# Regrouping the expert output matmuls of a windowed-attention and mixture-of-experts block: tiles in groups of 4 and 3

## The chip, the cores and the metric

The kernel runs on one core of a Trainium2 chip. The metric is device time in microseconds (us) of one execution. The engines are called by their names in the profile: PE is TensorE (PEld its weight loads), DVE is VectorE, ACT is ScalarE, POOL is GpSimd, SP is SyncE.

## What is computed

The input x is 32 images of 56 x 56 pixels with 96 channels. One block of a network is applied, cut here to what matters:

```python
# 1. attention in 7x7 windows of the shifted image, 12 heads of 8 channels
x = x + attention(ln(x)) @ w_proj.T + b_proj
# 2. mixture of 4 experts, the two best of each token, exact gelu
probs = softmax(ln(x) @ gate_w + gate_b); masked = top-2 of probs, renormalised
h = gelu(ln(x) @ w1[e] + b1[e])             # 96 -> 384, for each expert e
y = h @ w2[e] + b2[e]                       # 384 -> 96
x = x + sum over e of masked[e] * y[e]
```

All experts are computed for all tokens; the gate weighs their results. The change concerns y and the weighted sum.

## The kernel before

**Units.** A unit is a strip of two times 7 x 56 pixels: 784 tokens, 16 windows. There are 128 units, four to an image. Tokens lie on 112 partitions ("lanes") in 7 tiles of 112 tokens each. A loop step works on several units at once: `f` is the unit in its expert part, `a` the next one, in attention, `b` the one after, in its first norm and q/k/v. Each engine runs its own program in its own order, and semaphores tie them. Of the 128 steps, 127 have an `a`; the prologue runs the attention of unit 0 without any `f`.

**Order on PE in a step.** First the hidden layer of `f` (24 blocks of three matmuls, the first two of which belong to the step before). Then scores of pair 0 and eight passes n = 0 to 7, one for each pair of windows. A pass issues, in this order: `scores(n+1)`, `attend(n-1)`, `transpose_p(n)`, at n = 4 also `transpose1(b)` (7 transposes), then the expert groups that `GROUPS_AT[n]` lists, then `turn_o(n-1)`. At n = 0 some groups stand ahead of `scores(1)`. The last pair of each half, n + 1 = 3 and 7, has two mask matmuls more in its scores. Behind the passes come q/k/v of `b`, `project(a)`, the `LATE_GROUPS`, `transpose2(a)` with one q/k block of `b` in its middle, `hidden` blocks 0 and 1, and the gate's scores.

**Order on DVE in a pass.** `combine` of the groups in `COMBINES_AT[n]`, then `softmax_pair(n+1)` (row maximum L735, subtraction L739; it waits for `scores(n+1)`), then `normalise_o(n-1)` (reciprocal L746, product L750). PE's `turn_o(n-1)` waits for that product. At n = 1 to 3 DVE also does the statistics of a later unit's first norm. Behind the projection `residual` runs: residual sums and statistics of both parts (4 and 3 tiles), centring and scaling (L779, L786), on which `transpose2` waits, the low parts of the normed input `x2_low` (L814), and four combines among them.

**An expert group.** `experts(f, g)` multiplies n tiles of tokens with w2 of one expert. Each tile takes 9 matmuls of 96 columns (three chunks of 128 hidden channels, three products of high and low float16 parts: L1123, L1125, L1127), ahead of them stands one matmul for the bias, n x 96 columns wide (L1116). The result lies in the PSUM bank `Y_BANK[g]`; a group waits until the group before it in that bank has been combined. Groups of expert 0 need low parts made by DVE, later experts those made by POOL (`lo_done`). `combine(f, g)` on DVE (L891) multiplies by the gate into a slot of `y_gated` (four slots), `add` on POOL (L458) adds the slot to the residual, and `store` on SP waits for the last add. POOL's step lists the low parts L448, adds and the first norm in a fixed order. `PARTS` is the number of groups of an expert, `N_Y` that of a unit.

**Other waits on groups.** `transpose1(b)` waits for `gated` at 6, since it writes banks 5 and 6. `hidden` block 1 writes bank 7 and waits for `gated` at 11. ACT's `round_chunk` writes a slot of `g_hi` anew once the expert that read it is done (`PARTS * (chunk // CPE - 1)` groups).

Of the kernel before, what the change touches and what calls it, by code (L numbers as in the profile page):

```python
# [33 lines left out]
B, IMG, C = 32, 56, 96  # L34
# [6 lines left out]
EXPERTS, HID = 4, 384  # L41
CHUNKS = EXPERTS * HID // 128
CPE = HID // 128
# [3 lines left out]
LANES = 2 * IMG  # L47
# [9 lines left out]
def at(unit, per_unit, k=0):  # L57

    m, c = unit
    return m * (UPI * per_unit) + (c * per_unit + k)  # L60
# [39 lines left out]

GROUP_TILES = ((0, 2), (2, 2), (4, 3))
PARTS = len(GROUP_TILES)
GROUPS_AT = ((0, 1, 2), (3,), (4,), (5,), (), (6,), (7,), ())
COMBINES_AT = ((0, 1), (2,), (3,), (4,), (5,), (), (6,), (7,))
LATE_GROUPS = (8, 9, 10, 11)
STATS_AT = ((), (0, 1), (2, 3), (4, 5, 6), (), (), (), ())
ROUND_AT = ((), (6,), (7,), (8,), (), (9,), (10,), (11,))

# [1 line left out]
T1_AT = 4  # L112
X1_LOW_AT = ((), (), (), (), (), (0, 1), (2, 3), ())

Y_BANK = (5, 7, 6, 5, 7, 6, 7, 7, 7, 4, 7, 4)
B2_COLS = EXPERTS * 3 * C

N_T1, N_QK, N_V, N_S, N_PT, N_O, N_OT = 2, 4, 2, 8, 16, 8, 2
VW = HD + 1
# [3 lines left out]
N_PROJ, N_T2, N_H, N_Y = 2, 2, 24, PARTS * EXPERTS  # L123
# [15 lines left out]
def build(nc, x, packed, wp, consts, out, keys):  # L139
    ctx = ExitStack()  # L140
    with ctx:
        def sb(name, shape, dt=F32):
            return ctx.enter_context(nc.sbuf_tensor(name, shape, dt))
# [86 lines left out]
        g_sb = sb("g_sb", [128, CHUNKS, TOK])  # L230
        g_hi = sb("g_hi", [128, 2 * CPE, TOK + PAD], F16)
        g_lo = sb("g_lo", [128, 2 * CPE, TOK + PAD], F16)
        y_gated = sb("y_gated", [LANES, 4, 3 * C])


        s_const = sem("s_const")
# [169 lines left out]
        @block.gpsimd  # L406
        def _(pool):

            nc.gpsimd.memset(k_bd[:, :, :, :], 0.0).then_inc(s_zero, 1)
            nc.gpsimd.memset(v_bd[:, :, :], 0.0).then_inc(s_zero, 1)  # L410
            nc.gpsimd.memset(p_sb[:, :, :, :], 0.0).then_inc(s_zero, 1)
            for odd in range(2):
                pool.wait_ge(s_zero, 3 + odd)
                nc.gpsimd.memset(v_bd[NB * odd:NB * odd + WW, :, VW * odd + HD:VW * (odd + 1)], 1.0
                                 ).then_inc(s_zero, 1)

            def norm1(a):

                u = a[1] % UPI
                pool.wait_ge(var1_done, at(a, 1, 1))  # L420
                nc.gpsimd.tensor_tensor(rstd1[:, :], ve1[:, :], minus_half[0:LANES, :].broadcast_to([LANES, W]),
                                        ALU.pow).then_inc(rstd1_done, 1)
                if not first(a):
                    pool.wait_ge(t1_done, at(a, N_T1))
                wide = [LANES, W, C]
                nc.gpsimd.tensor_tensor(xn1[:, :, :], xa[:, u, :].rearrange("p (t c) -> p t c", c=C),
                                        mv1[:, :, 0:1].broadcast_to(wide), ALU.subtract
                                        ).then_inc(centre1_done, 1)
                pool.wait_ge(rstd1_done, at(a, 1, 1))
                pool.wait_ge(centre1_done, at(a, 1, 1))  # L430
                nc.gpsimd.tensor_tensor(xn1[:, :, :], xn1[:, :, :], rstd1[:, :].unsqueeze(2).broadcast_to(wide),
                                        ALU.mult).then_inc(norm1_done, 1)

            def rsqrt2(f):
                for k, (j0, n) in enumerate(((0, 4), (4, 3))):
                    pool.wait_ge(var2_done, at(f, 2, k + 1))
                    nc.gpsimd.tensor_tensor(rstd2[:, j0:j0 + n], ve2[:, j0:j0 + n],  # L437
                                            minus_half[0:LANES, :].broadcast_to([LANES, n]),
                                            ALU.pow).then_inc(rstd2_done, 1)

            def low_part(f, chunk):

                if chunk < 2 * CPE:
                    pool.wait_ge(hi_dve, at(f, N_ROUND, chunk + 1))
                else:
                    pool.wait_ge(hi_act, at(f, N_ROUND, chunk - 2 * CPE + 1))
                slot = chunk % (2 * CPE)
                nc.gpsimd.tensor_tensor(g_lo[:, slot, 0:TOK], g_sb[:, chunk, :], g_hi[:, slot, 0:TOK],  # L448
                                        ALU.subtract).then_inc(lo_done, 1)

            def add(f, u, g):

                e, j0, n = tiles_of(g)
                pool.wait_ge(gated, at(f, N_Y, g + 1))
                if g >= PARTS:
                    pool.wait_ge(comb_done, at(f, N_Y, g - PARTS + 1))
                slot = xr[:, u, j0 * C:(j0 + n) * C]
                nc.gpsimd.tensor_tensor(slot, y_gated[:, g % 4, 0:n * C], slot, ALU.add).then_inc(comb_done, 1)  # L458

            def prologue():  # L460
                pool.wait_ge(s_ready, 1)
                norm1((0, 0))
                norm1((0, 1))
                rsqrt2((0, 0))

            def step(f, a, b, u):
                for chunk in range(CPE, 2 * CPE):
                    low_part(f, chunk)
                for g in range(3):
                    add(f, u, g)  # L470
                if b is not None:
                    norm1(b)
                for chunk in range(2 * CPE, 3 * CPE):
                    low_part(f, chunk)
                    add(f, u, chunk - CPE)
                low_part(f, 9)
                low_part(f, 10)
                add(f, u, 6)
                low_part(f, 11)
                add(f, u, 7)  # L480
                if a is not None:
                    rsqrt2(a)

                    pool.wait_ge(norm2_done, at(a, 2, 2))
                for g in LATE_GROUPS:
                    add(f, u, g)

            schedule(pool, step, prologue)


# [138 lines left out]
        def _(dve):  # L629
# [124 lines left out]
            def residual(f, before=None):  # L754
# [37 lines left out]
                sums_of(*first_part)  # L792
                variances(*first_part)
                if before is not None:
                    combine(before, 8)
                sums_of(*second_part)
                if before is not None:
                    combine(before, 9)
                centre(*first_part)
                variances(*second_part)  # L800
                scale(*first_part)
# [1 line left out]
                scale(*second_part)  # L803
                x2_low(f, 0)
                if before is not None:
                    combine(before, 10)
                    combine(before, 11)
                x2_low(f, 1)

            def x2_low(f, k):  # L810
# [148 lines left out]
        def _(pe):  # L959
# [143 lines left out]
            def experts(f, g):  # L1103

                e, j0, n = tiles_of(g)
                if e == 0:
                    pe.wait_ge(lo_dve, at(f, CPE, CPE))
                else:
                    pe.wait_ge(lo_done, at(f, N_LO, CPE * e))
                if g < 3:  # L1110
                    pe.wait_ge(gelu_done, at(f, N_H, N_H - 2 + g))
                earlier = [i for i in range(g) if Y_BANK[i] == Y_BANK[g]]
                if earlier:
                    pe.wait_ge(gated, at(f, N_Y, max(earlier) + 1))
                y = y_bank(g)[:, 0:n * C]
                T.matmul(y, ones16[:, :], b2_16[:, e * 3 * C:e * 3 * C + n * C], start=True, stop=False,  # L1116
                         skip_group_check=True)
                for k in range(n):
                    cols = slice((j0 + k) * LANES, (j0 + k) * LANES + 128)
                    for c in range(CPE):  # L1120
                        slot, wc = e % 2 * CPE + c, slice((e * CPE + c) * C, (e * CPE + c + 1) * C)
                        outp = y[:, k * C:(k + 1) * C]
                        T.matmul(outp, g_hi[:, slot, cols], w2_hi[:, wc], start=False, stop=False,  # L1123
                                 skip_group_check=True)
                        T.matmul(outp, g_hi[:, slot, cols], w2_lo[:, wc], start=False, stop=False,  # L1125
                                 skip_group_check=True)
                        ins = T.matmul(outp, g_lo[:, slot, cols], w2_hi[:, wc], start=False,  # L1127
                                       stop=(c == CPE - 1), skip_group_check=True)
                ins.then_inc(y_done, 1)
# [11 lines left out]
            def attention(a, b, f=None):  # L1141


                for n in range(8):
                    groups = list(GROUPS_AT[n]) if f is not None else []
                    if n == 0 and groups:
                        experts(f, groups.pop(0))
                        experts(f, groups.pop(0))
                    if n < 7:
                        scores(a, n + 1)  # L1150
                    if n:
# [4 lines left out]
                    if n == T1_AT and b is not None:  # L1156
                        if f is not None:

                            pe.wait_ge(gated, at(f, N_Y, 6))
                        transpose1(b)  # L1160
                    for g in groups:
                        experts(f, g)
# [15 lines left out]
                hidden(a, (0,))  # L1178
                if f is not None:

                    pe.wait_ge(gated, at(f, N_Y, 11))
                hidden(a, (1,))
                gate_scores(a)

# [23 lines left out]
def _layout(w_qkv, b_qkv, w_proj, b_proj, rel_table, gate_w, gate_b, w1, b1, w2, b2):  # L1208
# [4 lines left out]
    wg = np.concatenate([gate_w, gate_b[None]], 0)  # L1213
    w1b = np.concatenate([w1.transpose(1, 0, 2).reshape(C, EXPERTS * HID), b1.reshape(1, -1)], 0)
    b2r = np.zeros((128, B2_COLS), f)
    b2r[0] = b2r[32] = np.repeat(b2, 3, 0).reshape(-1)

    col, row = np.arange(WW) // W, np.arange(WW) % W
    idx = (row[:, None] - row[None] + W - 1) * (2 * W - 1) + (col[:, None] - col[None] + W - 1)
# [54 lines left out]
```

## Time and profile before

| | |
|---|---|
| time, median of 3 runs | 6585.76 us (6585.39 to 6585.8) |
| time of the profiled run | 6582.02 us |
| its span, first to last instruction | 6580.2 us |
| PE busy | 6329.5 us, 96% of the span |
| PEld busy | 5075.5 us, 77% |
| DVE busy | 5021.6 us, 76% |
| ACT busy | 4719.7 us, 72% |
| POOL busy | 3763.3 us, 57% |
| DMA | mean 44 GB/s, hardware queue 14.4% of 16 engines |
| mean granted TensorE clock | 0.996 |

A steady step lasts 50.40 us, from one `scores(0)` (3004.69) to the next (3055.09). A row of the timeline has the start, the duration, the engine, the line of the kernel, and what was written from what; an "xcount" merges rows of one kind; a bracket at the end gives the idle time before it and what ended that. Matmul durations overlap, so PE's progress is read from the difference of two starts, not from a duration. A row of the view of stretches has the stretch, its length, the busy time and instruction count of PE, PEld, DVE, ACT and POOL, PE's granted clock, the DMA share and the GB/s.

### The profile page before, as it was taken

Reading aid. Unit: us, or ns where it says so; the run is one execution under the profiler, and the core shown is the slowest. Engines: PE = TensorE matmul, PEld = TensorE weight load, DVE = VectorE, ACT = ScalarE, POOL = GpSimd, SP = SyncE. Lnnn points to the kernel's source line nnn. Section 1 sums busy time; section 2 is a strip of 40 time slices with the busy share of each in tenths; the row PEclk is TensorE's granted clock in tenths of the full one; section 3 lists DMA queues with packets and bytes.
Section 4 is the critical chain, followed back from the end, with each engine's and each line's share of the span. In section 5 each row is a group of like instructions: output and inputs, shape, how many; then the busy total and the mean of one; then the engine's idle time right before and its main releaser. Section 6 shows DMA issues by size and latency. Waiting matters only on the chain.

```text
span 6580.2 us, 265098 instructions
## 1 busy us (share of the span) xinstructions
PE 6329.5 (96%) x99456; PEld 5075.5 (77%) x99456; DVE 5021.6 (76%) x15655; ACT 4719.7 (72%) x9087; POOL 3763.3 (57%) x3337
## 2 busy tenths in 40 slices
PE   5999999999999999999999999999999999999997
PEld 4777777777777777777777777777777777777776
DVE  5777777777777777777777777777777777777775
ACT  3777777777777777777777777777777777777775
POOL 2565555555555565556555555555565555555555
PEclk9999999999999999999999999999999999999999
DMA  1111111111111111111111111111111111111110
GB/s 57 44 43 44 46 45 43 44 46 44 45 42 46 44 44 44 45 43 44 44 46 43 44 45 45 43 45 45 44 43 45 46 44 43 44 46 45 45 41 24
DMA packets 190611, 290.00 MB, mean 44 GB/s; under 512 B 42450, under 2 KB 151634, under 8 KB 189266
## 3 DMA queue, kind: packets, MB, share of 16 engines
q1 hardware_dynamic: 189394, 273.23, 14.4%
q8 instruction: 831, 13.62, 0.9%
q14 instruction: 386, 3.16, 0.2%
HBM read 138.18 MB, written 77.07 MB: 33 GB/s over the span
## 4 chain that ended last, share of the span: by engine, by line
PE 73%; DVE 15%; issue 5%; ACT 4%; POOL 2%; SPq 1%; DVEq 0%; DMA 0%; ACTq 0%; POOLq 0%
PE ps_t L1036 10%; PE ps_o L1053 9%; PE ps_f L964 8%; PE ps_f L965 8%; PE ps_f L966 8%; PE ps_s L1016 5%; PE ps_s L1026 4%; PE ps_f L1127 3%; PE ps_f L1125 3%; PE ps_f L1123 3%; DVE s_max L735 3%; PE ps_o L1062 3%; POOL rstd L437 2%; DVE stat L766 2%; PE ps_t L983 2%
## 5 line engine op out<-in xcount | busy, mean ns | idle before, releaser
L448 POOL TENSOR_TENSOR g_lo<-g_sb,g_hi 128x784 f16<-128x784 f32 x1152 | 2014.9, 1758 | 1774.3 <-DVE g_hi L873 1013.8
L541 ACT ACTIVATE g_sb<-ps_f 128x392 f32<-128x392 f32 x3072 | 1525.9, 497 | 127.6 <-PE ps_f L966 126.8
L563 ACT ACTIVATE pt_sb<-ps_t 113x588 f32<-113x588 f32 x1024 | 677.4, 662 | 1077.8 <-PE ps_t L1036 1065.0
L735 DVE TENSOR_REDUCE s_max<-ps_s 113x12 f32<-113x588 f32 x1024 | 789.1, 771 | 746.9 <-PE ps_s L1026 746.9
L1127 PE MATMUL ps_f<-w_hi,g_lo 128*128 128x96 f16 x8832 | 1227.3, 206 | 0.0
L1125 PE MATMUL ps_f<-w_lo,g_hi 128*128 128x96 f16 x8832 | 1226.7, 206 | 0.0
L1123 PE MATMUL ps_f<-w_hi,g_hi 128*128 128x96 f16 x8832 | 1226.1, 206 | 0.0
L458 POOL TENSOR_TENSOR xr<-y_gated,xr 112x192 f32<-112x192 f32 (+1 forms) x1536 | 987.0, 660 | 374.6 <-DVE y_gated L891 275.7
L964 PE MATMUL ps_f<-x_hi,w_hi 128*128 128x392 f16 x3072 | 1012.2, 329 | 19.5 <-issue 5.3
L965 PE MATMUL ps_f<-x_lo,w_hi 128*128 128x392 f16 x3072 | 1010.7, 329 | 0.0
L966 PE MATMUL ps_f<-x_hi,w_lo 128*128 128x392 f16 x3072 | 1010.6, 329 | 0.0
L1036 PE MATMUL ps_t<-ident,p_sb 113*113 113x113 f32 x6144 | 854.6, 275 | 26.9 <-ACT p_sb L558 26.7
L1125 PEld LDWEIGHTS ps_f<-w_lo,g_hi 128*128 128x128 f16 x8832 | 862.9, 98 | 10.2
L1123 PEld LDWEIGHTS ps_f<-w_hi,g_hi 128*128 128x128 f16 x8832 | 865.2, 98 | 0.1
L1127 PEld LDWEIGHTS ps_f<-w_hi,g_lo 128*128 128x128 f16 x8832 | 863.5, 98 | 0.0
L739 DVE TENSOR_TENSOR s_sub<-ps_s,s_max 113x588 f32<-113x588 f32 x1024 | 790.0, 772 | 57.0
L1053 PEld LDWEIGHTS ps_o<-v_bd,pt_sb 113*49 113x49 f32 x24576 | 738.0, 125 | 114.1 <-ACT pt_sb L563 67.1
L1053 PE MATMUL ps_o<-v_bd,pt_sb 113*49 113x18 f32 x24576 | 785.5, 198 | 24.2 <-ACT pt_sb L563 20.2
L558 ACT ACTIVATE p_sb<-s_sub 113x588 f32<-113x588 f32 x1024 | 715.7, 699 | 77.6 <-DVE s_sub L739 72.6
L1036 PEld LDWEIGHTS ps_t<-ident,p_sb 113*113 113x113 f32 x6144 | 695.9, 178 | 80.4 <-issue 51.3
L534 ACT ACTIVATE g_hi<-g_sb 128x784 f16<-128x784 f32 x768 | 647.3, 843 | 3.1 <-PE ps_f L1127 3.1
L437 POOL TENSOR_TENSOR rstd<-ve,cst 112x4 f32<-112x4 f32 (+1 forms) x256 | 270.9, 1058 | 595.4 <-DVE ve L775 595.4
(132 smaller groups left out, 13415.6 us busy)
## 6 DMA issues: line engine op xcount, KB each, us to landing
k_bd<-keys SPq DMA_DIRECT2D x1536, 36.8 KB
q_st<-qk_hi SPq DMA_DIRECT2D x768, 49.0 KB, 1.9
xr<-x SPq DMA_DIRECT2D x224, 139.1 KB
out<-xr SPq DMA_DIRECT2D x224, 139.1 KB
xa<-x SPq DMA_DIRECT2D x224, 136.5 KB
keys<-qk_hi SPq DMA_DIRECT2D x128, 147.0 KB, 2.4
keys<-qk_lo SPq DMA_DIRECT2D x128, 147.0 KB, 2.8
q_st<-qk_lo SPq DMA_DIRECT2D x384, 49.0 KB, 2.0
```

The source lines that it names most:

```text
L448: nc.gpsimd.tensor_tensor(g_lo[:, slot, 0:TOK], g_sb[:, chunk, :], g_hi[:, slot, 0:TOK], ALU.subtract).then_inc(lo_done, 1)
L458: nc.gpsimd.tensor_tensor(slot, y_gated[:, g % 4, 0:n * C], slot, ALU.add).then_inc(comb_done, 1)
L541: nc.scalar.activation(g_sb[:, chunk, half * STRIP:(half + 1) * STRIP], h_bank[k % 3][:, 0:STRIP], ACT.Gelu, scale=1.0 / WSCALE).then_inc( ...
L735: V.tensor_reduce(s_max[:, :], scores, AX.X, ALU.max).then_inc(max_done, 1)
L964: T.matmul(outp, lhs_hi, rhs_hi, start=start, stop=False, skip_group_check=True)
L965: T.matmul(outp, lhs_hi, rhs_lo, start=False, stop=False, skip_group_check=True)
L966: return T.matmul(outp, lhs_lo, rhs_hi, start=False, stop=True, skip_group_check=True)
L1036: ins = T.transpose(bank[2 + p // 4][0:SPAN, (p % 4) * 128:(p % 4) * 128 + SPAN], p_sb[0:SPAN, n % 2, 2 * p:2 * p + 2, :].rearrange("p h k ...
L1053: ins = T.matmul(ps_o[NB * s:NB * s + WW, O0 + p * 2 * VW:O0 + (p + 1) * 2 * VW], pt_sb[0:SPAN, p, s * WW:(s + 1) * WW], v_bd[0:SPAN, win ...
L1123: T.matmul(outp, g_hi[:, slot, cols], w2_hi[:, wc], start=False, stop=False, skip_group_check=True)
L1125: T.matmul(outp, g_hi[:, slot, cols], w2_lo[:, wc], start=False, stop=False, skip_group_check=True)
L1127: ins = T.matmul(outp, g_lo[:, slot, cols], w2_hi[:, wc], start=False, stop=(c == CPE - 1), skip_group_check=True)
```

## The change

Each expert's 7 tiles are split into two groups, of 4 and 3 tiles, instead of three groups of 2, 2 and 3. A unit has 8 groups instead of 12. The number of tiles within the pairs stays at 18, that behind the projection at 10. By pass n = 0 to 7, the tiles were 7, 2, 2, 3, 0, 2, 2, 0 and become 7, 4, 3, 0, 0, 4, 0, 0; of the 7 at n = 0, 4 stand ahead of `scores(1)` in both. Behind the projection groups of 3, 2, 2 and 3 tiles become 3, 4 and 3. DVE's combines and POOL's adds follow; the combine that stood between the residual statistics of the second part and the centring of the first is gone from there, and the two behind the first `x2_low` have 4 and 3 tiles in place of 2 and 3. The semaphore counts, banks, the slots of `y_gated` and the layout of the bias follow.

```diff
--- before.py
+++ after.py
@@ -100,11 +100,11 @@
 
 
 
-GROUP_TILES = ((0, 2), (2, 2), (4, 3))
+GROUP_TILES = ((0, 4), (4, 3))
 PARTS = len(GROUP_TILES)
-GROUPS_AT = ((0, 1, 2), (3,), (4,), (5,), (), (6,), (7,), ())
-COMBINES_AT = ((0, 1), (2,), (3,), (4,), (5,), (), (6,), (7,))
-LATE_GROUPS = (8, 9, 10, 11)
+GROUPS_AT = ((0, 1), (2,), (3,), (), (), (4,), (), ())
+COMBINES_AT = ((0,), (1,), (2,), (3,), (), (), (4,), ())
+LATE_GROUPS = (5, 6, 7)
 STATS_AT = ((), (0, 1), (2, 3), (4, 5, 6), (), (), (), ())
 ROUND_AT = ((), (6,), (7,), (8,), (), (9,), (10,), (11,))
 
@@ -112,8 +112,8 @@
 T1_AT = 4
 X1_LOW_AT = ((), (), (), (), (), (0, 1), (2, 3), ())
 
-Y_BANK = (5, 7, 6, 5, 7, 6, 7, 7, 7, 4, 7, 4)
-B2_COLS = EXPERTS * 3 * C
+Y_BANK = (5, 7, 6, 5, 7, 7, 4, 7)
+B2_COLS = EXPERTS * 4 * C
 
 N_T1, N_QK, N_V, N_S, N_PT, N_O, N_OT = 2, 4, 2, 8, 16, 8, 2
 VW = HD + 1
@@ -230,7 +230,7 @@
         g_sb = sb("g_sb", [128, CHUNKS, TOK])
         g_hi = sb("g_hi", [128, 2 * CPE, TOK + PAD], F16)
         g_lo = sb("g_lo", [128, 2 * CPE, TOK + PAD], F16)
-        y_gated = sb("y_gated", [LANES, 4, 3 * C])
+        y_gated = sb("y_gated", [LANES, 4, 4 * C])
 
 
         s_const = sem("s_const")
@@ -466,18 +466,17 @@
             def step(f, a, b, u):
                 for chunk in range(CPE, 2 * CPE):
                     low_part(f, chunk)
-                for g in range(3):
-                    add(f, u, g)
+                add(f, u, 0)
                 if b is not None:
                     norm1(b)
+                add(f, u, 1)
                 for chunk in range(2 * CPE, 3 * CPE):
                     low_part(f, chunk)
-                    add(f, u, chunk - CPE)
-                low_part(f, 9)
-                low_part(f, 10)
-                add(f, u, 6)
-                low_part(f, 11)
-                add(f, u, 7)
+                add(f, u, 2)
+                add(f, u, 3)
+                for chunk in range(3 * CPE, CHUNKS):
+                    low_part(f, chunk)
+                add(f, u, 4)
                 if a is not None:
                     rsqrt2(a)
 
@@ -792,10 +791,8 @@
                 sums_of(*first_part)
                 variances(*first_part)
                 if before is not None:
-                    combine(before, 8)
+                    combine(before, 5)
                 sums_of(*second_part)
-                if before is not None:
-                    combine(before, 9)
                 centre(*first_part)
                 variances(*second_part)
                 scale(*first_part)
@@ -803,8 +800,8 @@
                 scale(*second_part)
                 x2_low(f, 0)
                 if before is not None:
-                    combine(before, 10)
-                    combine(before, 11)
+                    combine(before, 6)
+                    combine(before, 7)
                 x2_low(f, 1)
 
             def x2_low(f, k):
@@ -1113,7 +1110,7 @@
                 if earlier:
                     pe.wait_ge(gated, at(f, N_Y, max(earlier) + 1))
                 y = y_bank(g)[:, 0:n * C]
-                T.matmul(y, ones16[:, :], b2_16[:, e * 3 * C:e * 3 * C + n * C], start=True, stop=False,
+                T.matmul(y, ones16[:, :], b2_16[:, e * 4 * C:e * 4 * C + n * C], start=True, stop=False,
                          skip_group_check=True)
                 for k in range(n):
                     cols = slice((j0 + k) * LANES, (j0 + k) * LANES + 128)
@@ -1145,7 +1142,6 @@
                     groups = list(GROUPS_AT[n]) if f is not None else []
                     if n == 0 and groups:
                         experts(f, groups.pop(0))
-                        experts(f, groups.pop(0))
                     if n < 7:
                         scores(a, n + 1)
                     if n:
@@ -1156,7 +1152,7 @@
                     if n == T1_AT and b is not None:
                         if f is not None:
 
-                            pe.wait_ge(gated, at(f, N_Y, 6))
+                            pe.wait_ge(gated, at(f, N_Y, 4))
                         transpose1(b)
                     for g in groups:
                         experts(f, g)
@@ -1178,7 +1174,7 @@
                 hidden(a, (0,))
                 if f is not None:
 
-                    pe.wait_ge(gated, at(f, N_Y, 11))
+                    pe.wait_ge(gated, at(f, N_Y, 8))
                 hidden(a, (1,))
                 gate_scores(a)
 
@@ -1213,7 +1209,7 @@
     wg = np.concatenate([gate_w, gate_b[None]], 0)
     w1b = np.concatenate([w1.transpose(1, 0, 2).reshape(C, EXPERTS * HID), b1.reshape(1, -1)], 0)
     b2r = np.zeros((128, B2_COLS), f)
-    b2r[0] = b2r[32] = np.repeat(b2, 3, 0).reshape(-1)
+    b2r[0] = b2r[32] = np.repeat(b2, 4, 0).reshape(-1)
 
     col, row = np.arange(WW) // W, np.arange(WW) % W
     idx = (row[:, None] - row[None] + W - 1) * (2 * W - 1) + (col[:, None] - col[None] + W - 1)
```

## Rows read from the trace of the kernel before

**Rows 1.** Busy time by stretch: steady unit, then prologue pairs; columns in the text above.
```profile
3004.69:3055.09 50.40, 49.32 (x780) 39.56 (x779) 39.09 (x122) 36.88 (x72) 29.25 (x27) 1.00 0.15 44
89.00:101.50 12.50, 10.17 (x176) 8.39 (x176) 9.92 (x33) 7.00 (x15) 0.00 (x0) 1.00 0.01 3
```
**Rows 2.** Timeline, TensorE, steady unit, pairs 1 to 6: start us, duration us, engine, line.
```profile
3010.10 0.44 PE L1016 MATMUL ps_s<-bias,sel 128*64 128x392 f16 x4
...
3011.94 0.25 PE L1116 MATMUL ps_f<-b,ones 128*128 128x192 f16 x1
...
3013.14 0.36 PE L1016 MATMUL ps_s<-bias,sel 128*64 128x392 f16 x2
...
3015.24 0.25 PE L1116 MATMUL ps_f<-b,ones 128*128 128x192 f16 x1
...
3016.43 0.45 PE L1016 MATMUL ps_s<-bias,sel 128*64 128x392 f16 x4
...
3018.27 0.29 PE L1116 MATMUL ps_f<-b,ones 128*128 128x288 f16 x1
...
3019.54 0.27 PE L1062 MATMUL ps_o<-turn,o_tok 113*96 113x113 f32 x1
...
3019.74 0.45 PE L1016 MATMUL ps_s<-bias,sel 128*64 128x392 f16 x4
...
3022.78 0.44 PE L1016 MATMUL ps_s<-bias,sel 128*64 128x392 f16 x4
...
3024.86 0.25 PE L1116 MATMUL ps_f<-b,ones 128*128 128x192 f16 x1
...
3025.70 0.26 PE L1062 MATMUL ps_o<-turn,o_tok 113*96 113x113 f32 x1
...
3025.90 0.36 PE L1016 MATMUL ps_s<-bias,sel 128*64 128x392 f16 x2
...
3029.19 0.73 PE L1053 MATMUL ps_o<-v_bd,pt_sb 113*49 113x18 f32 x24
```
**Rows 3.** Timeline, TensorE, the prologue's pairs without expert groups.
```profile
89.04 0.45 PE L1016 MATMUL ps_s<-bias,sel 128*64 128x392 f16 x4
...
91.85 0.30 PE L1062 MATMUL ps_o<-turn,o_tok 113*96 113x113 f32 x1 [0.81 <-DVE o_tok L750]
...
92.08 0.44 PE L1016 MATMUL ps_s<-bias,sel 128*64 128x392 f16 x4
...
98.17 0.36 PE L1016 MATMUL ps_s<-bias,sel 128*64 128x392 f16 x2
...
101.22 0.30 PE L1062 MATMUL ps_o<-turn,o_tok 113*96 113x113 f32 x1 [0.80 <-DVE o_tok L750]
...
101.46 0.32 PE L1053 MATMUL ps_o<-v_bd,pt_sb 113*49 113x18 f32 x6
```
**Rows 4.** Timeline, VectorE, steady unit, pair 3: normalised output of pair 2.
```profile
3018.93 0.26 DVE L750 TENSOR_TENSOR o_tok<-ps_o,s_rec 113x96 f32<-113x96 f32 x1
```
**Rows 5.** Timeline, GpSimd, steady unit: last low part of expert 2.
```profile
3020.54 1.68 POOL L448 TENSOR_TENSOR g_lo<-g_sb,g_hi 128x784 f16<-128x784 f32 x1 [0.16 <-ACT g_hi L534]
```
**Rows 6.** Timeline, VectorE, steady unit, behind the projection.
```profile
3038.83 0.34 DVE L891 TENSOR_TENSOR y_gated<-ps_o,gate 112x192 f32<-112x192 f32 x1
...
3041.79 0.62 DVE L814 TENSOR_TENSOR x_lo<-ps_f,x_hi 96x448 f16<-96x448 f32 x1
...
3042.59 0.44 DVE L891 TENSOR_TENSOR y_gated<-ps_o,gate 112x288 f32<-112x288 f32 x1
...
3042.96 0.49 DVE L814 TENSOR_TENSOR x_lo<-ps_f,x_hi 96x336 f16<-96x336 f32 x1
```
**Rows 7.** Timeline, TensorE, steady unit, behind the late groups.
```profile
3040.59 0.59 PE L1079 MATMUL ps_f<-ident,xn 112*96 112x112 f32 x4
...
3042.97 0.33 PE L964 MATMUL ps_f<-x_hi,w_hi 128*128 128x392 f16 x1
...
3043.51 0.18 PE L964 MATMUL ps_s<-wg_hi,x_hi 128*128 128x4 f16 x1
```

## Prediction

> **What bounds the kernel now.** I read the busy times of one steady unit first. PE is busy 49.32 us of the unit's 50.40 us, DVE 39.09, ACT 36.88, POOL 29.25 [rows 1]. So PE sets the pace and only two things can move the time: how long PE needs for its instructions, and where it stands still between them. The second view is PE's timeline of the passes over the window pairs, read from start to start. It shows two kinds of pass. Some are as long as PE's own instructions; others are as long as a chain through DVE. That chain goes `scores(n+1)` on PE, row maximum and subtraction on DVE, reciprocal and product of the pair before on DVE, `turn_o(n-1)` on PE. In pass 3 it starts at 3016.43 [rows 2] and ends at 3018.93 + 0.26 = 3019.19 [rows 4], 2.76 us on. `turn_o` starts only at 3019.54 [rows 2], because the expert group of three tiles before it lasts longer. Here the chain is covered, by 0.35 us. The third view is the most telling one. The prologue runs the same passes without any expert group, so it shows the chain bare: from 89.04 to 91.85 PE gets to `turn_o` 2.81 us after the scores, having stood idle 0.81 us for the DVE product, and the next scores start at 92.08 [rows 3]. A pass without a group therefore lasts 3.04 us. With mask matmuls in its scores it lasts 3.29 us (98.17 to 101.46), with 0.80 us idle [rows 3].
>
> **The change, part by part.** First the price of a group on PE. Three tiles last 3019.54 - 3018.27 = 1.27 us, two tiles 3025.70 - 3024.86 = 0.84 us [rows 2]. A tile is 0.43 us and nothing measurable is left for the start of a group (0.84 less two tiles is -0.02). Four tiles are 1.27 + 0.43 = 1.70 us. Four bias matmuls a unit fewer, of the same columns in sum, are worth nothing by these rows; with the rounding of 0.02 us each, at most 0.08 us a unit, which is left to the range.
>
> Now the passes, each as (scores to group) + group + `turn_o`, the last being 0.20 us (3019.54 to 3019.74) [rows 2], and compared with the pass of before:
>
> - Pass 0: seven tiles in both kernels, four of them ahead of `scores(1)`: 0.
> - Pass 1, 2 tiles become 4. Scores to group is 3011.94 - 3010.10 = 1.84 us. New length 1.84 + 1.70 + 0.20 = 3.74. Old: 3013.14 - 3010.10 = 3.04. This is +0.70, less than two tiles (0.86), because the old pass was already waiting for the chain.
> - Pass 2, 2 become 3. Scores to group is 3015.24 - 3013.14 = 2.10 us. New 2.10 + 1.27 + 0.20 = 3.57, old 3016.43 - 3013.14 = 3.29: +0.28.
> - Pass 3, 3 become 0. Old 3019.74 - 3016.43 = 3.31. PE's own work in it would be 1.84 + 0.20 = 2.04, but the chain holds it at 3.04 [rows 3]: -0.27. Of 1.27 us of group taken out, 1.00 us becomes idle time.
> - Pass 4 has the transposes of the next unit and no group in either: 0.
> - Pass 5, 2 become 4. Scores to group is 3024.86 - 3022.78 = 2.08 us. New 2.08 + 1.70 + 0.20 = 3.98, old 3025.90 - 3022.78 = 3.12: +0.86.
> - Pass 6, 2 become 0. Old 3029.19 - 3025.90 = 3.29 [rows 2]. Bare, by the prologue, 3.29 [rows 3]: 0. The old pass was already at the chain's length, so taking the group out gives nothing.
> - Pass 7 has no group in either: 0.
>
> The passes sum to 0.70 + 0.28 - 0.27 + 0.86 = +1.57 us a unit [rows 2, 3]. The same tiles are done in the same order, but two passes now lack cover and stand at the chain, and their tiles lengthen passes that had nothing left to hide.
>
> Behind the projection PE's groups take the same ten tiles. The old fourth group had to wait for a combine on DVE; the new third one needs a combine that DVE does before it, so that stall goes. What is late next is the norm. `transpose2` starts at 3040.59 [rows 7], as soon as DVE has scaled. One combine of two tiles, at 3038.83, disappears from ahead of the centring: 0.34 us long, some 0.25 us from its start to the next instruction's [rows 6]. So `transpose2`, and the first `x2_low` behind it, come 0.25 us earlier, the latter at 3041.79 - 0.25 = 3041.54. But the tiles of that combine are done elsewhere. Between the start of `x2_low` and that of the last combine there are 3042.59 - 3041.79 = 0.80 us [rows 6]; two tiles more in the combine between them cost 0.10 us each by 0.34 us for two tiles and 0.44 us for three [rows 6], so the last combine starts at 3041.54 + 0.80 + 0.20 = 3042.54 and ends 0.44 us later, at 3042.98. This is what `hidden` block 1 now waits for, where before it waited for the smaller combine ahead of it. It started at 3042.97 and the gate's scores at 3043.51 [rows 7]; now it can start at about 3043.04, adding 0.05 us from a DVE end to PE (the chain ends 2.76 us after the scores, PE goes on 2.81 us after them). The second `x2_low` starts as before, within 0.04 us of 3042.96. So the 0.25 us are given back: I take +0.05 us a unit, between -0.25 (the head start stays) and +0.30 (a combine of four tiles, at most 0.54 us by the same slope, held against the 0.25).
>
> What costs nothing, and its cover: DVE has four combines fewer a unit and PE does not wait for DVE there; a combine of four tiles at passes 1, 2 and 6 stands ahead of the row maximum, which waits for scores anyway, and both engines have room in the unit [rows 1]. POOL's adds are four fewer. Its first norm moves ahead of two adds, three low parts of expert 2 come in a row ahead of two adds. The last of these low parts ended at 3020.54 + 1.68 = 3022.22 [rows 5], and the group that reads them started at 3024.86 [rows 2]: 2.6 us spare. ACT's rounding, which releases that low part, moves back 0.98 us with passes 1 and 2, the group only 0.71 us, and 2.3 us stay. If that cover were gone the group of pass 5 would wait, with PE's queue behind it. No wait is added on SP and no transfer is issued, moved or resized; the stores only follow the last add.
>
> Sum: 1.57 + 0.05 = 1.62 us a unit, in the 127 steps that have passes: 205.7 us. The last step, without passes, I take as unchanged. Against the profiled run 6582.02 + 205.7 = 6787.7 us. The median of the runs lies 3.7 us above the profiled run, which gives 6791 us, 3.1% slower.
>
> **A rule that bears on it.** In the prologue's passes, PE idled 0.8 us out of every 3.04 to 3.29 us and its granted clock read 1.00, the 2.4 GHz level [rows 1, 3]. The Trainium skill (TensorE: Matmul & The Clock Gate, "A second HAM failure mode: psum-queue depth-cycling") tells of a kernel in which frequent short idle times between groups of matmuls made the clock swing between its two levels. By that rule the new idle times would cost clock, which is rival 4 below; the row speaks against it.
>
> **The rivals.**
> (1) The chain is no bound: `turn_o` would be released earlier in passes 3 and 6, which then shrink to PE's own work, 2.04 us and 2.10 + 0.23 = 2.33 us. Pass 3 would give -1.27 and pass 6 -0.96, the passes in sum 0.70 + 0.28 - 1.27 + 0.86 - 0.96 = -0.39, with the late part -0.34 us a unit: 6586 - 43 = 6543 us, 0.7% faster than before. It decides when the DVE product of a bare pass ends less than 2.0 us after its scores start. For it speaks only that DVE is at 78% load; against it the two waits of 0.8 us in rows 3. Chance 0.04.
> (2) The head start behind the projection stays, because PE or ACT hides the later combines: 1.57 - 0.25 = 1.32 us a unit, 6586 + 168 = 6753 us. It would need block 1 of `hidden` not to wait for the last combine. Chance 0.09.
> (3) The late combines cost more, +0.30 us: 1.87 x 127 = 237, 6823 us. Chance 0.04.
> (4) The clock falls to 1.2 GHz behind the bare pass 3 and stays there for passes 4 and 5: these last 3.04 and 3.98 us, and at half the clock at most twice that, an estimate: +7.0 us a unit, 127 x 7.0 = 889, 7475 us. Chance 0.01.
> (5) The cover moves without net effect, the new idle time being offset by the stalls that go; that would need 1.6 us of old stalls in a unit that has 50.40 - 49.32 = 1.08 us of idle in all [rows 1]. Chance 0.02.
>
> **How the numbers follow.** The forecast, 6791 us, has 0.80; its own error of about 0.1 us a unit is 13 us either way. Range: from rival 2 less a little for the bias matmuls, 6750, to rival 3, 6825; left out are rivals 1, 4 and 5 and some error, some 0.1. A difference of 0.2% (13 us) is about what a measurement can tell from no change. Faster has 0.04 (rival 1), same 0.02 (rival 5), slower the rest, 0.94.
>
> **What would show it.** In the profile after: idle of about 1.0 us before `turn_o` released by the DVE product, twice a unit, in passes 3 and 6, so some 250 us of such waits in all; pass lengths 3.74, 3.57, 3.04, 3.04, 3.98, 3.29 us; a unit of 52.0 us; the late groups without a wait between them; `hidden` block 1 waiting for the last combine; clock still 1.00. The prediction is wrong if passes 3 and 6 are shorter than 3.0 us, if passes 1 or 5 grow by less than 0.6 us, or if a wait on POOL's low parts appears ahead of the group of pass 5.

## The result, and the profile after

The changed kernel takes 6783.29 us (median of 4 runs, 6783.15 to 6785.4) against 6585.78 us for the kernel before on the same chip (6585.39 to 6586.61): a ratio of 1.030, 95% interval 1.0283 to 1.0318. It is 198 us slower; 205 us were forecast.

From the page of the changed kernel, the span and the busy times:

```profile
span 6781.3 us, 261146 instructions
...
PE 6329.8 (93%) x98944; PEld 5024.2 (74%) x98944; DVE 5042.8 (74%) x15143; ACT 4717.4 (70%) x9087; POOL 3697.3 (55%) x2825
```

PE is busy for 6329.8 us, where it was 6329.5 us: its work is the same, and the whole loss is time in which it stands still. A steady unit in the view of stretches (length, busy PE, PEld, DVE, ACT, POOL, clock, DMA share, GB/s), to be read beside [rows 1]:

```profile
3044.92:3096.89 51.97, 49.28 (x775) 39.14 (x774) 39.20 (x118) 36.85 (x72) 29.17 (x24) 1.00 0.15 43
```

The unit has grown by 1.57 us (50.40 to 51.97), PE's busy time in it not at all. Over 127 units that is 199 us. Every fourth unit, in which the loop closes, is 0.32 us longer in both kernels. The passes, on PE's timeline of two neighbouring units (start, duration), to be read beside [rows 2]:

```profile
3050.32 0.45 PE L1013 MATMUL ps_s<-bias,sel 128*64 128x392 f16 x4
...
3052.16 0.33 PE L1113 MATMUL ps_f<-b,ones 128*128 128x384 f16 x1
...
3053.85 0.26 PE L1059 MATMUL ps_o<-turn,o_tok 113*96 113x113 f32 x1
3054.05 0.36 PE L1013 MATMUL ps_s<-bias,sel 128*64 128x392 f16 x2
...
3057.61 0.44 PE L1013 MATMUL ps_s<-bias,sel 128*64 128x392 f16 x4
...
3060.43 0.30 PE L1059 MATMUL ps_o<-turn,o_tok 113*96 113x113 f32 x1 [0.81 <-DVE o_tok L749]
3060.66 0.45 PE L1013 MATMUL ps_s<-bias,sel 128*64 128x392 f16 x4
...
3063.70 0.45 PE L1013 MATMUL ps_s<-bias,sel 128*64 128x392 f16 x4
```
```profile
3011.35 0.44 PE L1013 MATMUL ps_s<-bias,sel 128*64 128x392 f16 x4
...
3015.32 0.36 PE L1013 MATMUL ps_s<-bias,sel 128*64 128x392 f16 x2
...
3018.38 0.30 PE L1059 MATMUL ps_o<-turn,o_tok 113*96 113x113 f32 x1 [0.80 <-DVE o_tok L749]
3018.61 0.73 PE L1050 MATMUL ps_o<-v_bd,pt_sb 113*49 113x18 f32 x24
```

The lengths are 3.73, 3.56, 3.05 and 3.04 us for passes 1 to 4 (first fence, scores to scores), 3.97 and 3.29 us for passes 5 and 6 (second fence). The two brackets are the bare chain of [rows 3] in the steady unit: 0.81 us idle in pass 3, 0.80 us in pass 6, each ended by the DVE product. In the sums of waits (total us, times, longest), the two rows on this product were, before and then after:

```profile
PEld ps_o L1062 <- DVE o_tok L750: 50.3, 133, 1.0
PE ps_o L1062 <- DVE o_tok L750: 3.8, 6, 0.8
...
PEld ps_o L1059 <- DVE o_tok L749: 300.4, 387, 1.0
PE ps_o L1059 <- DVE o_tok L749: 208.4, 260, 0.8
```

The weight load of `turn_o` (PEld) waited once a unit before, for 0.4 us; two waits a unit of 1.0 us are new. The matmul itself (PE) hardly waited before and now waits twice a unit for 0.8 us, 204.6 us more in all. PE's idle time as a whole (span less busy time) grew by 200.8 us, from 250.7 to 451.5: these waits are the loss. Behind the projection, PE's timeline, beside [rows 7]; `project` started at 3023.88, in the unit of the old rows at 3034.46. The first row below is from before, the others from after:

```profile
3034.46 1.61 PE L1068 MATMUL ps_f<-wp_sb,o_sb 128*112 128x96 f32 x14
...
3023.88 1.61 PE L1065 MATMUL ps_f<-wp_sb,o_sb 128*112 128x96 f32 x14
...
3029.76 0.59 PE L1076 MATMUL ps_f<-ident,xn 112*96 112x112 f32 x4
...
3032.46 0.34 PE L961 MATMUL ps_f<-x_hi,w_hi 128*128 128x392 f16 x1 [0.16 <-DVE y_gated L888]
...
3032.97 0.17 PE L961 MATMUL ps_s<-wg_hi,x_hi 128*128 128x4 f16 x1
```

Counted from `project`, `transpose2` starts 0.25 us earlier (5.88 us in place of 6.13), block 1 of `hidden` 0.07 us later (8.58, was 8.51), the gate's scores 0.04 us later (9.09, was 9.05). The bracket names what took the head start back: the last late combine. The sums of waits balance here: the late group's wait for a combine (23.2 us, 127 times) is gone, and block 1's wait for the last combine (20.0 us, 127 times) is new.

### The profile page after: what moved, and what is told of

Same layout as the page of the kernel before. It is cut to its first block, busy times and chain, and to the rows that moved or that the text cites. A ratio compares the mean times of both kernels' runs of the same rounds, so it can differ in the third digit from the quotient of the medians.

```text
span 6781.3 us, 261146 instructions
## 1 busy us (share of the span) xinstructions
PE 6329.8 (93%) x98944; PEld 5024.2 (74%) x98944; DVE 5042.8 (74%) x15143; ACT 4717.4 (70%) x9087; POOL 3697.3 (55%) x2825
## 4 chain that ended last, share of the span: by engine, by line
PE 65%; DVE 20%; issue 8%; ACT 4%; POOL 2%; DMA 0%; DVEq 0%; SPq 0%; ACTq 0%; POOLq 0%
PE ps_f L961 8%; PE ps_f L963 7%; PE ps_f L962 7%; PE ps_t L1033 7%; PE ps_o L1050 6%; DVE s_max L734 6%; PE ps_s L1013 5%; PE ps_s L1023 4%; PE ps_f L1124 3%; PE ps_f L1122 3%; PE ps_f L1120 3%; PE ps_o L1059 3%; POOL rstd L437 2%; DVE stat L765 2%; PE ps_t L980 2%
## 5 line engine op out<-in xcount | busy, mean ns | idle before, releaser
L1124 PE MATMUL ps_f<-w_hi,g_lo 128*128 128x96 f16 x9216 | 1248.1, 206 | 0.0
L1122 PE MATMUL ps_f<-w_lo,g_hi 128*128 128x96 f16 x9216 | 1247.6, 206 | 0.0
L1120 PE MATMUL ps_f<-w_hi,g_hi 128*128 128x96 f16 x9216 | 1247.2, 206 | 0.0
L458 POOL TENSOR_TENSOR xr<-y_gated,xr 112x384 f32<-112x384 f32 (+1 forms) x1024 | 907.1, 896 | 411.3 <-DVE y_gated L888 295.7
L1122 PEld LDWEIGHTS ps_f<-w_lo,g_hi 128*128 128x128 f16 x9216 | 901.9, 98 | 39.1
L1120 PEld LDWEIGHTS ps_f<-w_hi,g_hi 128*128 128x128 f16 x9216 | 903.3, 98 | 0.1
L1124 PEld LDWEIGHTS ps_f<-w_hi,g_lo 128*128 128x128 f16 x9216 | 902.1, 98 | 0.0
L888 DVE TENSOR_TENSOR y_gated<-ps_f,gate 112x288 f32<-112x288 f32 (+1 forms) x896 | 445.5, 497 | 232.2 <-PE ps_f L1124 231.8
```

## Experiments

Every ratio is against the kernel before, measured on the same chip: its median was 6585.6 us beside the first four, 6587.6 us beside the next three, 6586.7 us beside the last. The edits are shown shortened (banks, counts, combines and adds follow the groups): the first, second and fourth against the kernel before, the third and sixth against the changed kernel, the fifth against the fourth, the last against the seventh.

### Placement without large groups

```diff
-GROUPS_AT = ((0, 1, 2), (3,), (4,), (5,), (), (6,), (7,), ())
-LATE_GROUPS = (8, 9, 10, 11)
+GROUPS_AT = ((0, 1, 2), (3, 4), (5,), (), (), (6,), (), ())   # expert 2: 4 and 3 tiles, the others 2, 2, 3
+LATE_GROUPS = (7, 8, 9, 10)
```

> Only the placement of the changed kernel: passes 0 to 7 have 7, 4, 3, 0, 0, 4, 0, 0 tiles, but the groups stay small: the four tiles of pass 1 are two groups of two, the three late groups of expert 3 stay 2, 2 and 3 (only expert 2 has 4 and 3, since its four tiles of pass 5 find one free bank). The part behind the projection is that of before. If the loss comes from where the tiles stand (my theory), the passes last 3.73, 3.56, 3.05, 3.04, 3.97 and 3.29 us (passes 1 to 6), +1.55 us a unit over before, and the time is 6586 + 197 = 6783 us, within 5 us. If it comes from the size of the groups (wider bias matmuls, combines and adds), most of the 198 us is absent: under 6650 us.

Measured: 6793.0 us (5 runs, 6790.9 to 6797.4), ratio 1.0316 (1.0302 to 1.0330). The pass lengths are 3.73, 3.56, 3.05, 3.04, 3.97 and 3.29 us, those of the changed kernel to 0.01 us, and a unit lasts 51.95 us. Pass 1 in its timeline, now with two groups of two tiles:

```profile
3002.29 0.25 PE L1119 MATMUL ps_f<-b,ones 128*128 128x192 f16 x1
...
3003.14 0.25 PE L1119 MATMUL ps_f<-b,ones 128*128 128x192 f16 x1
...
3003.99 0.27 PE L1065 MATMUL ps_o<-turn,o_tok 113*96 113x113 f32 x1
```

Two groups of two last 1.70 us, as one of four does (3052.16 to 3053.85, 1.69 us). The placement alone makes the whole loss, and with 11 groups in place of 8 nothing of it comes back. The size of the groups was varied in pass 1 and behind the projection and is worth nothing in pass 1; pass 5 kept its group of four, so there it was not tested. The time itself is 10 us above the expected 6783, beyond the 5 us allowed: the units that are not disturbed are as expected, and what is added is told under the next experiment.

### One move: pass 6 to pass 5

```diff
-GROUPS_AT = ((0, 1, 2), (3,), (4,), (5,), (), (6,), (7,), ())
+GROUPS_AT = ((0, 1, 2), (3,), (4,), (5,), (), (6,), (), ())   # group 6 has four tiles
```

> One move alone: the two tiles of pass 6 are done in pass 5, joined with the two there; passes 1 to 3 and the part behind the projection as before. My theory: pass 6 was already at the length of the chain (3.29 us) and gives nothing back, pass 5 goes from 3.12 to 3.97 us: +0.85 us x 127 = 108 us, 6694 us. If a pass without a group shrank to PE's own work, pass 6 would give back 0.96 us: 6586 - 14 = 6572 us.

Measured: 6707.8 us (4 runs, 6705.0 to 6710.6), ratio 1.0185 (1.0169 to 1.0200): +122 us, where 108 were expected and -14 by the rival. Passes 1 to 6 last 3.04, 3.29, 3.31, 3.04, 3.97 and 3.29 us: pass 5 grew by 0.85 us and pass 6 gave nothing back. An undisturbed unit lasts 51.26 us, +0.86, which makes 109 us. The other 13 us are not in the passes. Stretches of this kernel, an ordinary unit and one that isn't, then single microseconds in the second:

```profile
3063.89:3115.15 51.26, 49.37 (x777) 39.45 (x777) 39.07 (x121) 36.85 (x72) 29.11 (x26) 1.00 0.15 43
...
3217.99:3270.63 52.64, 50.91 (x777) 40.53 (x777) 39.16 (x121) 36.85 (x72) 29.58 (x27) 0.97 0.15 43
```
```profile
3242.00:3243.00 1.00, 0.31 (x4) 0.12 (x2) 0.96 (x3) 0.66 (x2) 0.09 (x1) 1.00 0.01 5
3243.00:3244.00 1.00, 0.90 (x26) 0.76 (x26) 0.62 (x3) 1.00 (x3) 0.00 (x0) 1.00 0.04 8
3244.00:3245.00 1.00, 1.00 (x8) 0.74 (x5) 0.49 (x2) 0.33 (x1) 0.59 (x1) 0.55 0.00 0
3245.00:3246.00 1.00, 1.00 (x7) 1.00 (x6) 0.28 (x1) 0.49 (x1) 1.00 (x1) 0.50 0.00 0
```

In 3242 to 3243 PE stands idle for 0.80 us, waiting for the product in pass 6; one microsecond later the granted clock reads 0.55 and then 0.50, the 1.2 GHz level, for 3.4 us in all, and this unit lasts 1.38 us longer. From unit 1 to unit 126 of this kernel the clock falls so in 10 units, in the kernel above in 7, in the next one in 4, in the changed kernel in one (unit 45). Ten times 1.38 us are 14 us, the missing 13; seven times are 10 us, what the experiment above had too much. Each of these 22 falls comes 1.7 to 2.1 us after the start of the wait of 0.80 us in pass 6, none behind a bare pass 2 or 3. In the same part the kernel before has a single fall, in unit 125, behind an idle time of 1.7 us, and the kernels of the later experiments, which have no such wait in pass 6, have none. So the long wait in pass 6 goes with the falls; why only a few of these waits are followed by one, and why their number differs between kernels with the same passes, stays open. The Trainium skill (TensorE: Matmul & The Clock Gate, "A second HAM failure mode: psum-queue depth-cycling") tells of a kernel in which frequent short idle times between groups of matmuls make the clock swing between its two levels. These rows agree in so far as the clock falls behind a short idle time, but in 10 of 127 units at most.

### The same tiles spread evenly

```diff
-GROUPS_AT = ((0, 1), (2,), (3,), (), (), (4,), (), ())
+GROUPS_AT = ((0, 1), (2,), (), (3,), (), (4,), (), ())
```

> The changed kernel with its group of three tiles moved from pass 2 to pass 3, so that groups stand in passes 1, 3 and 5, evenly. My theory: what counts is how many passes have no group at all, each of which leaves about 0.96 us idle; there are two either way, so the sum of the passes is 3.73 + 3.29 + 3.31 + 3.04 + 3.97 + 3.29 us against 3.73 + 3.56 + 3.05 + 3.04 + 3.97 + 3.29 us, the same within 0.02 us: 6782 us, within 5 us of the changed kernel. Rival: an even spread lets the engines recover between groups, which should be worth a part of the loss, 6700 to 6760 us.

Measured: 6788.0 us (5 runs, 6786.2 to 6792.2), ratio 1.0309 (1.0295 to 1.0323), as the changed kernel. Passes 1 to 6 last 3.73, 3.29, 3.31, 3.04, 3.97 and 3.29 us, the unit 51.96 us. Pass 2 gave up 0.27 us and pass 3 took it. The even spread is worth nothing: three groups in the five passes 1, 2, 3, 5 and 6 leave two bare in either order. (Which of them are bare was varied only between 2 and 3.) The 5 us above the changed kernel are at the edge of what was expected; this kernel's four falls of the clock, at 1.38 us, account for them.

### The part behind the projection alone

```diff
-                if before is not None:
-                    combine(before, 9)
                 centre(*first_part)
...
-                    combine(before, 10)
-                    combine(before, 11)
+                    combine(before, 9)    # four tiles
+                    combine(before, 10)   # three tiles
```

> Only the part behind the projection as in the changed kernel: groups and passes of before, but expert 3 has groups of 4 and 3, late groups are 3, 4 and 3 tiles and the combine between the statistics and the centring is gone. My theory: transpose2 starts 0.25 us earlier, and hidden block 1 waits for the last combine and gives it back: +0.04 us a unit, 6591 us, 6586 to 6596. Rival (the head start stays): -0.25 us a unit, 6554 us.

Measured: 6585.5 us (11 runs, 6583.6 to 6589.2), ratio 1.0000 (0.9991 to 1.0009). The median is half a microsecond below the expected 6586 to 6596, so the time alone cannot be told from no change; the rows below tell more. A unit lasts 50.43 us, +0.03. The rival's -32 us is out. PE's timeline from `transpose2` on; `project` started at 3040.70:

```profile
3046.57 0.59 PE L1080 MATMUL ps_f<-ident,xn 112*96 112x112 f32 x4
...
3049.27 0.34 PE L965 MATMUL ps_f<-x_hi,w_hi 128*128 128x392 f16 x1 [0.16 <-DVE y_gated L892]
3049.78 0.17 PE L965 MATMUL ps_s<-wg_hi,x_hi 128*128 128x4 f16 x1
```

5.87, 8.57 and 9.08 us behind `project`: the numbers of the changed kernel. The 0.25 us come and go as forecast, with no pass changed.

### The late combine in the gap

```diff
                 centre(*second_part)
+                if before is not None:
+                    combine(before, 9)
                 scale(*second_part)
                 x2_low(f, 0)
                 if before is not None:
-                    combine(before, 9)
                     combine(before, 10)
                 x2_low(f, 1)
```

> Passes as before, late groups of 3, 4 and 3 tiles, and the combine of four tiles stands ahead of the second scaling, where DVE waits 0.45 us for POOL's power in every unit, instead of behind the first low part. My theory: the head start of 0.25 us then stays, less the 0.05 to 0.1 us by which this combine overfills the gap: -0.15 to -0.20 us a unit, 6560 to 6567 us. If the combines behind the first low part don't hold hidden block 1, the move is worth nothing or costs the 0.1 us: 6590 to 6600 us.

Measured: 6544.6 us (5 runs, 6543.4 to 6546.5), ratio 0.9935 (0.9921 to 0.9948): faster than the kernel before by 43 us, more than the 20 to 27 expected. A unit lasts 50.10 us, -0.30, which makes 38 of the 43 us; the other 5 are not in the units, and their cause is open. DVE's timeline:

```profile
3026.31 0.45 DVE L781 TENSOR_TENSOR xn<-xr,mv 112x288 f32<-112x288 f32 x1
3026.68 0.55 DVE L892 TENSOR_TENSOR y_gated<-ps_o,gate 112x384 f32<-112x384 f32 x1
3027.21 0.46 DVE L788 TENSOR_TENSOR xn<-xn,rstd 112x288 f32<-112x288 f32 x1
```

From the centring to the scaling there are 0.90 us (3026.31 to 3027.21), and in the changed kernel, where this place was empty, 3029.62 to 3030.51, 0.89 us as well. The combine of four tiles is free there: I had priced it by its full duration of 0.55 us against a gap of 0.45 us, but its start overlaps the end of the instruction before it, and from its start to the next there are only 0.53 us. So the head start stays, and the gate's scores come 8.75 us behind `project`, 0.30 us earlier than before.

### Reciprocal and product ahead of the subtraction

```diff
-            def softmax_pair(a, n):
+            def softmax_pair(a, n, between=None):
...
                 V.tensor_reduce(s_max[:, :], scores, AX.X, ALU.max).then_inc(max_done, 1)
+                if between is not None:
+                    between()
...
-                        softmax_pair(a, n + 1)
+                        softmax_pair(a, n + 1, (lambda n=n: normalise_o(a, n - 1)) if n else None)
...
-                    if n:
+                    if n == 7:
                         normalise_o(a, n - 1)
```

> The changed kernel with one order on DVE turned: reciprocal and product of the pair before stand between the row maximum and the subtraction, not behind both. My theory: the idle time of the passes without a group ends with the DVE product, so turn_o comes at once and the next scores wait for the subtraction instead, 2.75 to 2.8 us after the last: passes 3 and 6 lose 0.25 us each, the passes with four tiles nothing, and pass 5 may lose 0.15 us to a later save of the output on ACT: -0.35 to -0.5 us a unit, 6720 to 6740 us. If those passes are bound by something else, no change: 6783 us.

Measured: 6710.8 us (4 runs, 6708.1 to 6715.0), ratio 1.0186 (1.0170 to 1.0202), 72 us below the changed kernel and beyond the 43 to 63 us expected. A unit lasts 51.35 us, -0.62. Passes 1 to 6 last 3.73, 3.57, 2.69, 2.70, 4.33 and 3.01 us. PE's timeline from pass 3 on:

```profile
3031.16 0.30 PE L1061 MATMUL ps_o<-turn,o_tok 113*96 113x113 f32 x1
3031.84 0.45 PE L1015 MATMUL ps_s<-bias,sel 128*64 128x392 f16 x4 [0.38 <-DVE s_sub L740]
...
3035.64 0.73 PE L1052 MATMUL ps_o<-v_bd,pt_sb 113*49 113x18 f32 x24 [0.39 <-ACT o_sb L573]
...
3041.88 0.73 PE L1052 MATMUL ps_o<-v_bd,pt_sb 113*49 113x18 f32 x24 [0.46 <-ACT pt_sb L562]
```

`turn_o` of pass 3 now comes without a wait of PE, 2.01 us after its scores (3029.15 to 3031.16), and the next scores wait 0.38 us for the subtraction. That confirms the chain and its order: the product was the last link, the subtraction is the next. It was worth 0.36 us in pass 3, 0.28 us in pass 6 (3038.87 to 3041.88), and 0.34 us in pass 4, which I had taken for bound by PE; it was at the chain as well, the two being level. Pass 5 gave 0.36 us back (3.97 to 4.33), since `attend` there waits for ACT's save of the output, and `attend` of pair 6 waits for ACT's copy. Together the passes changed by -0.61 us, which is the unit's -0.62. ACT's order is the next thing behind DVE's.

### Both, on the groups of before

The edits of the two experiments before, on the kernel with 11 groups.

> The groups and passes of before, late groups of 3, 4 and 3 tiles with the combine of four in the gap ahead of the second scaling, and the DVE order with reciprocal and product between maximum and subtraction. My theory: the three old waits of 0.11 to 0.12 us for the product in passes 1, 2 and 6 go (-0.34 us), pass 5 gives back up to 0.15 us, the late part brings -0.15 to -0.20: -0.35 to -0.5 us a unit, 6522 to 6542 us, faster than both kernels. If the passes of before are bound by PE alone, only the late part's 20 to 25 us: 6560 us.

Measured: 6488.6 us (4 runs, 6487.9 to 6493.6), ratio 0.9852 (0.9837 to 0.9867): 99 us faster than the kernel before, where 46 to 66 were expected. Most units last 49.66 us, -0.74, those in which the loop closes 49.98 us. Passes 1 to 5: 2.89, 3.14, 3.31, 2.71 and 3.47 us against 3.04, 3.29, 3.31, 3.04 and 3.12 before. The old waits of passes 1 and 2 are gone and were worth 0.15 us each, as was that of pass 6; pass 4 gains 0.33 us, which the expectation did not have, and pass 5 gives 0.35 us back, where 0.15 was the most expected; the part behind the projection brings 0.30 us in place of 0.15 to 0.20. The scores and `attend` of pass 5:

```profile
3031.56 0.45 PE L1019 MATMUL ps_s<-bias,sel 128*64 128x392 f16 x4
...
3032.65 0.73 PE L1056 MATMUL ps_o<-v_bd,pt_sb 113*49 113x18 f32 x24 [0.38 <-ACT o_sb L576]
```

### The save ahead of the exponential

```diff
                     copy_pt(a, n)
+                    if n == 4:
+                        save_o(a, 0)
                     if n < 7:
                         exps(a, n + 1)
...
-                    if n == 4:
-                        save_o(a, 0)
```

> The fastest kernel so far (groups and passes of before, the late combine of four tiles in the gap, reciprocal and product ahead of the subtraction) with one order on ACT turned: in pass 4 the save of the first half of the attention output stands ahead of the exponential of pair 5, not behind it. In that kernel pass 4 shrank from 3.04 to 2.71 us, but pass 5 grew from 3.12 to 3.47 us, with attend waiting 0.5 us for that save. My theory: the save ends about 0.4 us earlier, attend waits about 0.1 us, and the exponential, now later, is just in time for the transposes of pair 5: pass 5 lasts 3.15 to 3.25 us, -0.22 to -0.32 us a unit, 6448 to 6461 us. Rival: the exponential now holds the transposes instead and takes all of it back: 6485 to 6492 us.

Measured: 6441.6 us (5 runs, 6441.1 to 6449.0), ratio 0.9784 (0.9771 to 0.9797): 47 us below the last one, faster than the kernel before by 2.2%, and 6 us beyond the best expected. Pass 5 is back at 3.12 us; a unit lasts 49.30 us, -0.36. PE's timeline of passes 4 and 5, then ACT's:

```profile
3057.86 0.45 PE L1020 MATMUL ps_s<-bias,sel 128*64 128x392 f16 x4
3058.60 0.73 PE L1057 MATMUL ps_o<-v_bd,pt_sb 113*49 113x18 f32 x24
```
```profile
3058.05 0.49 ACT L576 ACTIVATE o_sb<-ps_o 96x392 f32<-96x392 f32 x1 [0.19 <-PE ps_o L1066]
3058.44 0.70 ACT L560 ACTIVATE p_sb<-s_sub 113x588 f32<-113x588 f32 x1
```

`attend` starts 0.74 us after its scores, where it was 3032.65 - 3031.56 = 1.09 us, and the exponential, though later, is in time: it ends at 3059.14, and the transposes that read it start at 3059.26 without a wait.

## Why the prediction was right, point by point

**The bound.** That PE sets the pace and that a bare pass is as long as the chain through DVE held in both bare passes: 3.05 us and 3.29 us, idle 0.81 and 0.80 us [rows 3]. The prologue's rows could be carried to the steady unit unchanged, and moving the last link of the chain moved the bound. The signs named for it came too: the new waits number two a unit (1.0 us on the weight load, 0.8 us on PE; 250.1 us more in all on the weight load), the late groups wait no longer, block 1 of `hidden` waits for the last combine, and PE waits for POOL's low parts twice in the whole run, for 3.8 us together.

**The passes.** Forecast 3.74, 3.57, 3.04, 3.04, 3.98 and 3.29 us, measured 3.73, 3.56, 3.05, 3.04, 3.97 and 3.29. The sum of the changes was forecast as +1.57 us and is +1.55. The step that carried the sign, that pass 6 gives nothing back, was shown alone: +0.85 us and no return.

**The price of a group.** A group's start was taken as worth nothing; two groups of two and one of four last the same within 0.01 us, measured in pass 1.

**Behind the projection.** +0.05 us was forecast. The changed kernel's unit grew by 1.57 us, its passes by 1.55, so this part takes 0.02 us; alone it measured 0.03. The head start of 0.25 us and the combine that takes it back were both as told.

**The size.** 1.62 us a unit were forecast and 1.57 came; 127 times 0.05 us are 6 of the 8 us by which 6791 is too high. The other 2 us come from the step from the profiled run to the median, taken as 3.7 us, where it was 6783.29 - 6783.15 = 0.1 us for the changed kernel; nearly 2 us of that are offset outside the ordinary units.

**The rivals.** Rival 1 fell with the one move, rivals 2 and 3 with the late part alone, rival 5 with the time. Rival 2's head start is real, and stays once the combine stands in the gap. Rival 4, the clock, was half right: a fall in every unit was priced and given 0.01. The clock does fall behind a bare pass, but behind pass 6 and not pass 3, and in few units: in one of the changed kernel, so it is not seen in its time, and in 7 and 10 in two of its relatives, where it costs 10 and 14 us. The row of the prologue that the prediction set against this rival spans 12.5 us with four bare passes and is too short for so rare an event. Why the changed kernel, with two bare passes a unit, falls less often than one with a single bare pass is open; it wasn't tried.

**What was wrong in the expectations of the experiments:** pass 4 was left out of both sums on the DVE order, as bound by PE's transposes, while it stood at the chain as well (0.33 us); the save of the output on ACT was expected to cost pass 5 0.15 us and cost 0.35; a combine was priced by its duration and not from start to start; and the falls of the clock were not foreseen (10 and 13 us).

## What to carry to other kernels

When tiles of filler work are moved between passes of a pipeline, count for each pass how long its dependency chain is bare and how long the engine's own work is: a pass is as long as the longer of the two, so filler taken out below the chain's length returns nothing, and filler added costs its whole length less what the pass still waited. A prologue or an epilogue in which the filler is missing shows the bare chain and prices this before anything is built. The number of filler groups did not make the loss here, nor did their size where it was varied: 11 groups placed as the 8 are lose the same 1.55 us a unit, and the starts that were saved were worth nothing. What large groups do is to leave fewer pieces than there are passes to cover, so check the coverage pass by pass before joining them.

## What the runs showed of the hardware that I had not expected

In the kernel with the one move, behind a wait of PE of 0.80 us in pass 6, the granted clock fell to its 1.2 GHz level in 10 of 127 units, for 3.4 us and a loss of 1.38 us each time. Behind waits of the same length in passes 2 and 3 it never fell. And on DVE a combine of 0.55 us fitted a wait of 0.44 us at no cost, since neighbours overlap: from the start of the centring to that of the scaling there were 0.90 us with it and 0.89 us without.
